# A half's worth of recurrence layers moved on by two in a fused recurrence and mixture-of-experts kernel on one core

## The chip, the cores and the metric

The kernel runs as one program on one core of a Trainium2 chip. The metric is the device time of one execution in microseconds (us); for several runs their median is given. Five engines work side by side, each on its own instruction stream: TensorE (PE in the profile; its weight loads are PEld), VectorE (DVE), ScalarE (ACT), GpSimd (POOL) and SyncE (SP), which here only issues DMA transfers. They wait for each other through semaphores.

## The reference

Two layers on `x` of 4 sequences x 1024 tokens x 1024 channels in float32. Each layer has a recurrence over the tokens (forwards and backwards) whose keys and values are both the `side` input and whose receptance is `x`, and a feed-forward part.

```python
# k = v = side, r = x; per channel: decay from w and cond
ek = exp(min(k, 30)); ekv = ek * v
a = a * decay + ekv_t          # numerator scan, forwards (nf) and backwards (nb)
b = b * decay + ek_t           # denominator scan (df, db)
euk = exp(min(u + k, 30))
num = nf + nb - ekv + euk * v
den = df + db - ek + euk
out = sigmoid(r) * num / max(den, 1e-8) * (0.8 + 0.2 * tf)

x = x + linear(recurrence_0(x, side)) # 1024x1024, scaled per output, with bias
r = recurrence_1(x, side)
h = rmsnorm(r) * norm_w
routed = top-4 of 32 experts on h (w1 1024x(2x512), silu(g) * u, w2 512x1024)
shared = (silu(h @ sg) * (h @ su)) @ sd
x = x + r + routed + shared
```

So num/den of both layers needs only `side`. The first layer's recurrence is also gated with `sigmoid(x)` of the input; the second one's sigmoid can only be applied when the first layer's x is known, so the kernel computes its quotient (called ratio) ahead of it.

## The kernel before, in words

**Products.** Every float32 product is made of three products of fp32r halves (a high and a low part of either operand). The 4096 tokens are worked off in eight *halves* of 512 tokens (`HALVES`). A half has 32 *steps* (`STEPS`); a step is one product of a 128-wide output block, 24 matmuls of 128x512. Steps 0, 1, 2, 4, 6, 8, 10, 11 (`STEP_L`) are the eight output blocks of the first layer's linear, steps 3, 5, 7, 9 and 12 to 15 (`STEP_D`) the eight blocks of the *previous* half's shared down product, steps 16 to 31 the gate and up products of the shared feed-forward. Half 0 has no previous half. `fill(h, i)` (L1482) is what an engine does in step i of half h. DVE's share is: at step_l(o)+1 the product's result is added to x (`XL`, L1505), at step_l(o)+2 the ratio is multiplied by the sigmoid (`C1`, L1498), at step_d(o)+1 the down product is taken in (`down`, L1455) and the residual sum is made (L1513). At step 16 the RMS root is taken (`root`, L1460 to L1468), then the eight blocks are normalised (`normalize`, L1477) and their low parts split (L1439); PE, which has summed the squares (L1696), transposes (L1706), computes the router's logits (L1708) and goes on with step 16.

**Recurrence layers.** The recurrences of both layers are cut into 32 *units*, a unit being one sequence and one block of 128 channels, 1024 tokens long; unit u is channel block u mod 8 of sequence u/8. A unit has two recurrence layers, l=0 (gated, written to `gated_dram`) and l=1 (ratio, written to `ratio_dram`), which share the side and its exponential EK and the product EKV = EK * side. A layer is on DVE: the denominator's forward scan F, the numerator's forward scan G, both backward scans, the term W = exp(u+k) in between, then two Newton operations on the inverse (which ACT starts by a Relu, Ln, Exp chain) and the scaling with it (`scaled`, L1094; with the gate multiply L1099 where l=0). POOL clips the side (L613), ACT takes its exponential (`side_exp`, L702).

**Order.** The order is written out by hand in `with_halves` (one list of calls per engine). The first eight units (`ALONE`) run in `alone`, before half 0 and next to the splitting of 32 pieces of shared weights on PE and ACT, four pieces a unit. There the EKV multiply is L1119, the scans are L1128, L1132, L1135 and L1145, the end of ACT's inverse chain is L833, L837, L839, and each unit's x is loaded to one buffer `X` by ACT's queue (L879) when the gate of the unit before is done. The other 24 units run in `unit`, four per half in halves 0 to 5 and always two halves ahead of their use: each unit's two layers are laid between eight steps of the half, with `fill(i)` calls at fixed places:

```python
for h in range(1, HALVES - 2):
    for q in range(UNITS_PER_HALF):
        u = h * UNITS_PER_HALF + ALONE + q
        unit(u, q % 2, lambda i: fill(h, q * FILLS_PER_UNIT + i, ...), prompt(u), not prompt(u - 1))
```

A *slot* below is one of the eight layers of a half, with four steps each; in DVE's `unit`, l=0 (even slots) has `fill(0)` ahead of the first scan and `fill(1)` behind it, l=1 has `fill(4)` behind its first scan and `fill(5)` only behind its scans and the scaling. The scaling is put off into the next layer, since the numerator's sum is made by an accumulating DMA that POOL issues (`add_numerator`); only the last unit of a sequence (`prompt`) scales at once. The next side is loaded by ACT's queue (`load_side`, L707) after the gate multiply of the layer before, x by L720.

**Half 6** has no units. DVE does the first part of the router's ranking there (`route_early`: `rank_start` at step 0, four `rank`s of six operations, L1242 to L1247, at steps 2, 4, 6, 8, the rest from step 19 on), and POOL then writes the routing entries as 112 small indirect DMAs (`put_entries`, L604) behind step 29 of half 6. Half 7 and the loop over the experts (L1822, L1836) follow.

## Time and profile before

| | |
|---|---|
| time, median of 3 runs (lowest, highest) | 4742.23 us (4740.93, 4744.61) |
| the profiled execution's own time | 4735.88 us |
| its span | 4734.2 us |
| its mean granted TensorE clock | 0.973 of full speed |
| PE busy | 4476.6 us (95%) |
| DVE busy | 2502.9 us (53%) |
| ACT busy | 1794.9 us (38%) |
| POOL busy | 834.6 us (18%) |

The profile is of one execution. The span runs from its first to its last instruction; the execution's own time is 1.7 us longer. Times in the rows are counted from the span's start. A busy share over the whole span is a mean over stages that are bound by different engines, so the section with the rows reads it by stage.

### The profile page before, as it was taken

Reading aid. Unit: us, or ns where it says so; the run is one execution under the profiler, and the core shown is the slowest. Engines: PE = TensorE matmul, PEld = TensorE weight load, DVE = VectorE, ACT = ScalarE, POOL = GpSimd, SP = SyncE. Lnnn points to the kernel's source line nnn. Section 1 sums busy time; section 2 is a strip of 40 time slices with the busy share of each in tenths; the row PEclk is TensorE's granted clock in tenths of the full one; section 3 lists DMA queues with packets and bytes.
Section 4 is the critical chain, followed back from the end, with each engine's and each line's share of the span. In section 5 each row is a group of like instructions: output and inputs, shape, how many; then the busy total and the mean of one; then the engine's idle time right before and its main releaser. Section 6 shows DMA issues by size and latency. Waiting matters only on the chain.

```text
span 4734.2 us, 60632 instructions
## 1 busy us (share of the span) xinstructions
PE 4476.6 (95%) x19926; PEld 3553.3 (75%) x19927; DVE 2502.9 (53%) x2708; ACT 1794.9 (38%) x2597; POOL 834.6 (18%) x992
## 2 busy tenths in 40 slices
PE   6778999999999946999999999999999999999999
PEld 2346787777778734778888888888888888888887
DVE  8999999999998411433143333444432143233432
ACT  6655555555554301232132323333331142222331
POOL 4410100101000062111111111111211111111211
PEclk9988999999999967999999999999999999999999
DMA  6777888988888624564254453655643345444443
GB/s 254 271 239 233 278 293 270 302 269 289 280 253 301 208 79 137 201 248 111 58 168 107 122 161 89 221 159 153 202 132 89 62 142 186 115 111 111 146 128 62
DMA packets 253977, 857.11 MB, mean 181 GB/s; under 512 B 28832, under 2 KB 61728, under 8 KB 229024
## 3 DMA queue, kind: packets, MB, share of 16 engines
q1 hardware_dynamic: 172944, 572.77, 34.1%
q0 software_dynamic: 53776, 182.09, 18.0%
q10 hardware_dynamic: 27136, 100.67, 5.6%
q8 instruction: 71, 1.16, 0.1%
q14 instruction: 50, 0.41, 0.0%
HBM read 652.40 MB, written 181.01 MB: 176 GB/s over the span
## 4 chain that ended last, share of the span: by engine, by line
PE 83%; issue 4%; DVE 3%; DMA 2%; ACT 0%; POOL 0%; POOLq 0%; DVEq 0%; ACTq 0%
PE ps L1822 33%; PE ps L1686 26%; PE ps L1836 16%; PE ps L1755 3%; PE ps L1708 1%; PE ps L1811 1%; PE ps L1696 1%; DMA work<-rows_dram,row_idx 1%; PE ps L1706 1%; PE ps L1722 1%; DVE halves L1558 0%; DVE work L1178 0%; DVE work L1195 0%; DVE work L1169 0%; DVE halves L1446 0%
## 5 line engine op out<-in xcount | busy, mean ns | idle before, releaser
L1822 PE MATMUL ps<-halves 128*128 128x512 f32 x7152 | 1695.5, 393 | 3.5 <-DVE halves L1563 2.8
L1686 PE MATMUL ps<-halves 128*128 128x512 f32 x6144 | 1469.6, 397 | 114.3 <-issue 106.2
L1822 PEld LDWEIGHTS ps<-halves 128*128 128x128 f32 x7152 | 1336.9, 189 | 278.4 <-DVE halves L1563 3.1
L1686 PEld LDWEIGHTS ps<-halves 128*128 128x128 f32 x6144 | 1159.2, 189 | 401.5 <-issue 159.0
L1836 PE MATMUL ps<-halves 128*128 128x512 f32 x3576 | 834.9, 389 | 1.3 <-DVE halves L1579 1.3
L1836 PEld LDWEIGHTS ps<-halves 128*128 128x128 f32 x3576 | 671.1, 188 | 140.9 <-DVE halves L1579 1.6
L1563 DVE TENSOR_TENSOR halves<-ps,halves 128x1024 fp32r<-128x1024 f32 x150 | 183.7, 1225 | 902.5 <-ACT halves L985 902.5
L594 POOL DMA_INDIRECT out<-work,add_idx x149 | 249.8, 1677 | 1420.4 <-DVE work L1585 1219.8
L1558 DVE TENSOR_TENSOR halves<-work,halves 128x1024 fp32r<-128x1024 f32 (+1 forms) x320 | 440.2, 1433 | 83.5 <-ACT halves L989 83.5
L985 ACT ACTIVATE halves<-ps 128x1024 fp32r<-128x1024 f32 x150 | 154.0, 1027 | 859.6 <-PE ps L1822 859.6
L989 ACT ACTIVATE halves<-work 128x1024 fp32r<-128x1024 f32 (+1 forms) x320 | 369.1, 1229 | 67.7 <-PE ps L1836 57.3
L1579 DVE TENSOR_TENSOR halves<-ps,halves 128x256 fp32r<-128x256 f32 x298 | 112.3, 419 | 491.5 <-ACT halves L1019 491.5
L1019 ACT ACTIVATE halves<-ps 128x256 fp32r<-128x256 f32 x298 | 98.6, 383 | 544.2 <-PE ps L1811 544.2
L1585 DVE TENSOR_SCALAR work<-ps,acc 128x512 f32<-128x512 f32 x149 | 111.6, 749 | 276.4 <-PE ps L1836 266.5
L1025 ACT ACTIVATE work<-ps,acc 128x512 f32<-128x512 f32 x149 | 102.1, 685 | 408.5 <-PE ps L1836 388.5
L613 POOL TENSOR_SCALAR work<-work 128x1024 f32<-128x1024 f32 x33 | 112.4, 3405 | 698.2 <-DMA work<-side_t 603.6
L584 POOL DMA_INDIRECT work<-rows_dram,row_idx x151 | 151.9, 1006 | 122.0 <-POOL row_idx L580 62.7
L1755 PE MATMUL ps<-ident,work 128*128 128x128 f32 x1200 | 158.4, 276 | 12.0 <-DMA work<-rows_dram,row_idx 12.0
L604 POOL DMA_INDIRECT slots_dram<-acc x128 | 124.5, 973 | 237.8 <-DVE acc L1319 199.4
L1755 PEld LDWEIGHTS ps<-ident,work 128*128 128x128 f32 x1200 | 137.8, 143 | 13.1 <-DMA work<-rows_dram,row_idx 13.0
L579 POOL COPY acc<-work (+1 forms) x151 | 48.9, 324 | 484.4 <-PE ps L1755 470.7
L696 ACT ACTIVATE work<-work,ones 128x512 f32<-128x512 f32 (+1 forms) x160 | 129.6, 810 | 5.2
(222 smaller groups left out, 3798.7 us busy)
## 6 DMA issues: line engine op xcount, KB each, us to landing
halves<-split_dram SPq DMA_DIRECT2D x512, 512.0 KB
work<-expert_w SPq DMA_DIRECT2D x192, 1024.0 KB, 5.6
split_dram<-halves ACTq DMA_DIRECT2D x32, 1024.0 KB, 5.2
plain<-shared_w SPq DMA_DIRECT2D x32, 512.0 KB, 3.4
work<-side_t ACTq DMA_DIRECT2D x32, 512.0 KB, 6.7
gated_dram<-work ACTq DMA_DIRECT2D x32, 512.0 KB, 5.1
work<-x_t ACTq DMA_DIRECT2D x32, 512.0 KB, 5.7
ratio_dram<-second ACTq DMA_DIRECT2D x32, 512.0 KB, 5.1
```

Source lines behind the costliest of these rows:

```text
L584: pool.indirect_dma_start(hx, None, rows_dram[:, :], bass.IndirectOffsetOnAxis(row_idx[:, :].bitcast(u32), 0)).then_inc(s["rows_in"], 16)
L594: pool.indirect_dma_start(out[:, :], bass.IndirectOffsetOnAxis(add_idx[:, :].bitcast(u32), 0), y, None, compute_op=ALU.add).then_inc(s["y_ ...
L604: pool.indirect_dma_start(slots_dram[:, :], bass.IndirectOffsetOnAxis(where[:, t * TOPK + k:t * TOPK + k + 1].bitcast(u32), 0), entry[:, 2 ...
L696: sc.activation(place, place, ACT.Ln, bias=ones[:, 0:1]).then_inc(s[steps], 1)
L985: sc.activation(xhi, ps_xt[:, :], ACT.Copy).then_inc(s["x_hi"], 1)
L989: sc.activation(whi[q][:, part], staged(q, part), ACT.Copy).then_inc(s["w1_hi" if q < 4 else "w2_hi"], 1)
L1558: ve.tensor_tensor(wlo[q][:, part], staged(q, part), whi[q][:, part].bitcast(f32), ALU.subtract)\
L1563: ve.tensor_tensor(xlo, ps_xt[:, :], xhi.bitcast(f32), ALU.subtract).then_inc(s["x_lo"], 1)
L1686: last = pe.matmul(bank(k % 4), w, op[:, part], start=(c == 0 and w is w_hi and op is hi), stop=(c == CB - 1 and w is w_lo))
L1755: last = pe.transpose(ps_xt[:, c * P:(c + 1) * P], hx[:, c * P:(c + 1) * P], ident[:, :])
L1822: last = pe.matmul(ps_h[:, a * 512:a * 512 + 512], xp[:, xk * P:(xk + 1) * P], wp[:, rhs], start=(xk == 0 and xp is xhi and wp is whi[q]), ...
L1836: last = pe.matmul(ps_y[:, h * 512:h * 512 + 512], ap_[:, (q * 2 + k) * P:(q * 2 + k + 1) * P], wp[:, rhs:rhs + 512], start=(q == 0 and k ...
```

## The change

The order of the recurrence layers becomes a table `JOBS` of (unit, layer). The unit is no longer the piece that is worked off, the layer (*job*) is.

- Fourteen jobs run before half 0, not sixteen: the second layers of units 4 and 5 are left out there. Every half takes eight jobs, in the slots 0 to 7: the second layers of the previous group's first two units (slots 0, 1), the first layers of this group's first two (2, 3), then both layers of the third (4, 5) and of the fourth (6, 7). The last two second layers run in steps 0 to 7 of half 6.
- A unit whose layers are apart has its side loaded, clipped and exponentiated twice (`SIDE_FIRST`): 46 times in all for 32 before. In slots 0 to 3 EK is multiplied in place into EKV (`single`, L1258), behind the first scan; elsewhere L1268 does it.
- Every job that opens a side has `fill(0)` ahead of and `fill(1)` behind its first scan; slots 5 and 7 keep the order of a second layer.
- Channel blocks 4 to 7 of a sequence are processed as 6, 7, 4, 5 (`UNIT_OF`, with the inputs permuted to match on the host), and the linear's contraction and `ratio_step` follow it.
- In the opening x has two buffers (`x_alone`), and is loaded a unit ahead; jobs 1, 3, 5 and 7 split three weight pieces, the other jobs two (`SPLIT_AT`).
- The ranks of half 6 move from steps 2, 4, 6, 8 to 12, 13, 14, 17 (`RANK_AT`), `rank_start` to step 11, the zeros' memset and store to steps 8 and 10.

```diff
+FILLS_PER_JOB = FILLS_PER_UNIT // 2
...
+LATE = UNITS_PER_HALF // 2
+UNIT_OF = (0, 1, 2, 3, 6, 7, 4, 5)
...
+def has_late_layer(u):
+
+    return u >= UNITS_PER_HALF and u % UNITS_PER_HALF < LATE
...
+JOBS = [(u, l) for u in range(ALONE) for l in range(2) if not (l and has_late_layer(u))]
+JOBS_ALONE = len(JOBS)
+JOBS_PER_HALF = 2 * UNITS_PER_HALF
+for first in range(ALONE, BLOCKS, UNITS_PER_HALF):
+    JOBS += [(first - UNITS_PER_HALF + q, 1) for q in range(LATE)]
+    JOBS += [(first + q, 0) for q in range(LATE)]
+    JOBS += [(first + q, l) for q in range(LATE, UNITS_PER_HALF) for l in range(2)]
+JOBS += [(BLOCKS - UNITS_PER_HALF + q, 1) for q in range(LATE)]
...
+SIDE_FIRST = [n for n, (u, l) in enumerate(JOBS) if l == 0 or has_late_layer(u)]
...
-    return STEP_L[o - 4] + 3 if o >= 4 else o // 2
+    return (STEP_L[0] + 3, STEP_L[1] + 3, STEP_L[5], STEP_L[7])[o - 4] if o >= 4 else o // 2
...
+RANK_AT = (12, 13, 14, 17)
...
+        def single(n):
+
+            return n >= JOBS_ALONE and slot(n) < 2 * LATE
...
+            for n in range(JOBS_ALONE):
+                u, l = JOBS[n]
+                if u < ALONE - 1:
+                    alone(n, lambda i: None)
+                else:
+                    alone(n, lambda i: fill(-1, STEPS - FILLS_PER_UNIT + i, first=False, prev=False, next_=True))
+            for n in range(JOBS_ALONE, len(JOBS)):
+                h, q = divmod(n - JOBS_ALONE, JOBS_PER_HALF)
+                job(n, lambda i: fill(h, q * FILLS_PER_JOB + i, first=h == 0, prev=h > 0, next_=True))
...
+                if l == 0 and u and not last:
+                    sc.wait_ge(s["gated"], u + 1)
+                    load_x(u + 1)
...
+                if l == 0 and has_late_layer(u):
+                    side_exp(SIDE_AT[n + 1])
...
+                def numerator_forward():
+                    if single(n):
+                        ve.wait_ge(s["h_fwd"], n + 1)
+                        ve.tensor_tensor(EK, EK, side, ALU.mult).then_inc(s["ekv"], 1)
...
+                if opens_side:
+                    fill(0)
+                    ve.wait_ge(s["ek"], i + 1)
...
+                ve.tensor_tensor_scan(F, d, EK, 0.0, ALU.mult, ALU.add).then_inc(s["h_fwd"], 1)
+                if prompt(n):
+                    numerator_forward()
+                else:
+                    fill(1 if opens_side else 0)
...
+                if not prompt(n):
+                    numerator_forward()
+                if pending(n):
+                    scaled(n - 1, W_of[1 - n % 2], N)
+                if prompt(n) or not opens_side:
+                    fill(1)
...
-                if i in (2, 4, 6, 8):
...
+                if i in RANK_AT:
```

What moves on DVE is seen in slot 3 of half 2, steps 12 and 13 (in the first order, of before, the second layer of the half's second unit). L1169 is the denominator's forward scan, L1178 its backward scan, L1167 the numerator's forward scan, L1094 and L1099 the scaling and the gate multiply of the layer before; L1498, L1505, L1455 and L1513 are the steps' work on PE's results.

```order
L1169 SCALAR_TENSOR_TENSOR work<-decay,work 128x1024
L1498 TENSOR_TENSOR plain<-work,more 128x512
L1505 SCALAR_TENSOR_TENSOR work<-ps,lsb,work 128x512
L1178 SCALAR_TENSOR_TENSOR work<-decay,edge_in,work 128x1024
L1167 SCALAR_TENSOR_TENSOR work<-decay,work 128x1024
L1094 SCALAR_TENSOR_TENSOR work<-work,neg_gain 128x1024
L1099 TENSOR_TENSOR work<-work 128x1024
L1455 TENSOR_TENSOR work<-ps,work 128x512
L1498 TENSOR_TENSOR plain<-work,more 128x512
L1513 SCALAR_TENSOR_TENSOR work<-work,lsb,plain 128x512
L1191 SCALAR_TENSOR_TENSOR work<-second,cap,work 128x1024
```

And in the changed kernel, where these are L1269, L1276, L1262, L1183, L1188, and L1591, L1598, L1548, L1606 for the steps' work; L1258 is the new multiply:

```order
L1269 SCALAR_TENSOR_TENSOR work<-decay,work 128x1024
L1548 TENSOR_TENSOR work<-ps,work 128x512
L1591 TENSOR_TENSOR plain<-work,more 128x512
L1606 SCALAR_TENSOR_TENSOR work<-work,lsb,plain 128x512
L1276 SCALAR_TENSOR_TENSOR work<-decay,edge_in,work 128x1024
L1258 TENSOR_TENSOR work<-work 128x1024
L1262 SCALAR_TENSOR_TENSOR work<-decay,work 128x1024
L1183 SCALAR_TENSOR_TENSOR work<-work,neg_gain 128x1024
L1188 TENSOR_TENSOR work<-work 128x1024
L1285 SCALAR_TENSOR_TENSOR work<-second,cap,work 128x1024
```

The three operations on a down product (L1455, L1498, L1513) stood behind both scans and the scaling; they (L1548, L1591, L1606) now stand right behind the first scan, and the multiply is added between the other two scans.

The second place is ACT's in the opening, behind a first layer of a unit. Before (L833 to L839 is the inverse, L715 the ratio's store, L798 a weight piece's high part, L815 and L821 the next layer's edges, L827 its exponential, L702 the exponential of the next unit's side):

```order
L833 ACTIVATE work<-ps,neg_low 128x1024
L837 ACTIVATE work<-work,low 128x1024
L839 ACTIVATE work<-work 128x1024
L715 DMA ratio_dram<-second 128x1024
L798 ACTIVATE halves<-plain 128x2x512 x2
L815 ACTIVATE edge_in<-work,edge 128x1
L821 ACTIVATE edge_in<-work,edge 128x1
L827 ACTIVATE work<-work,uu 128x1024
L702 ACTIVATE work<-work 128x1024
```

In the changed kernel behind job 9, the first layer of unit 5 (L942 to L948 is the inverse, L799 a result's store, L790 and L786 the loads of x and side, L781 the exponential of the side):

```order
L942 ACTIVATE work<-ps,neg_low 128x1024
L946 ACTIVATE work<-work,low 128x1024
L948 ACTIVATE work<-work 128x1024
L799 DMA gated_dram<-work 128x1024
L790 DMA work<-x_t 128x1024
L781 ACTIVATE work<-work 128x1024
L897 ACTIVATE halves<-plain 128x2x512 x2
L786 DMA work<-side_t 128x1024
L807 ACTIVATE edge_in<-work,edge 128x1
L815 ACTIVATE edge_in<-work,edge 128x1
```

The side's exponential stood in the next layer, behind its edges; it now stands behind the last operation of the inverse.

## Rows read from the trace of the kernel before

**Rows 1.** The busy tenths of the span in 40 slices, PE and DVE

```profile
PE   6778999999999946999999999999999999999999
...
DVE  8999999999998411433143333444432143233432
```

**Rows 2.** Busy time by stretch: us, PE, PEld, DVE, ACT, POOL (count), PEclk, DMA share, GB/s

```profile
17.90:286.40 268.50, 208.35 (x448) 89.54 (x449) 252.82 (x147) 174.06 (x196) 103.30 (x24) 0.92 0.71 264
286.40:480.30 193.90, 160.80 (x647) 119.40 (x646) 181.14 (x156) 112.58 (x157) 18.06 (x11) 0.90 0.71 233
...
1081.20:1282.60 201.40, 198.50 (x869) 155.17 (x869) 190.59 (x172) 117.81 (x167) 19.64 (x12) 1.00 0.84 282
...
1691.30:1827.10 135.80, 30.72 (x53) 14.89 (x53) 4.18 (x7) 4.67 (x7) 92.81 (x96) 0.52 0.09 24
...
591.00:680.60 89.60, 87.93 (x392) 72.44 (x390) 83.17 (x70) 52.87 (x74) 8.21 (x4) 1.00 0.86 295
680.60:778.70 98.10, 97.72 (x428) 77.96 (x429) 92.19 (x82) 54.30 (x75) 9.31 (x6) 1.00 0.88 287
```

**Rows 3.** Timelines of DVE, ACT, POOL, opening: start, us, operation, count [idle before]

```profile
144.69 1.20 DVE L1119 TENSOR_TENSOR work<-work 128x1024 f32<-128x1024 f32 x1
...
160.42 2.27 DVE L1128 TENSOR_TENSOR_SCAN work<-decay,work 128x1024 f32<-128x1024 f32 x1
...
164.79 3.06 DVE L1135 TENSOR_TENSOR_SCAN work<-decay,edge_in,work 128x1024 f32<-128x1024 f32 x1
...
209.55 1.20 DVE L1119 TENSOR_TENSOR work<-work 128x1024 f32<-128x1024 f32 x1
...
235.37 2.35 DVE L1135 TENSOR_TENSOR_SCAN work<-decay,edge_in,work 128x1024 f32<-128x1024 f32 x1 [5.64 <-ACT edge_in L815]
...
161.18 1.06 ACT L839 ACTIVATE work<-work 128x1024 f32<-128x1024 f32 x1
...
223.42 1.06 ACT L694 ACTIVATE work<-work 128x1024 f32<-128x1024 f32 x1 [5.98 <-DMA work<-x_t]
...
162.87 4.56 POOL L613 TENSOR_SCALAR work<-work 128x1024 f32<-128x1024 f32 x1 [14.36 <-DVE work L1128]
```

**Rows 4.** Timeline of DVE, half 0, where steps 7 and 8 meet

```profile
333.46 0.69 DVE L1498 TENSOR_TENSOR plain<-work 128x512 f32<-128x512 f32 x1 [2.27 <-issue]
```

**Rows 5.** Timeline of DVE, half 2, from step 13's slot to the normalised blocks

```profile
753.82 2.34 DVE L1178 TENSOR_TENSOR_SCAN work<-decay,edge_in,work 128x1024 f32<-128x1024 f32 x1
...
760.69 0.68 DVE L1455 TENSOR_TENSOR work<-ps,work 128x512 f32<-128x512 f32 x1
...
770.39 1.28 DVE L1205 SCALAR_TENSOR_TENSOR work<-work,low 128x1024 f32<-128x1024 f32 x1 [1.73 <-ACT work L754]
...
774.24 0.68 DVE L1460 TENSOR_SCALAR work<-ps 128x512 f32<-128x512 f32 x1
...
777.22 1.41 DVE L1477 SCALAR_TENSOR_TENSOR work<-plain,nrm,work 128x512 f32<-128x512 f32 x2
```

**Rows 6.** Timeline of PE, half 2: behind step 12, and at the transposes

```profile
758.42 1.02 PE L1696 MATMUL ps<-work,ones 128*128 128x512 f32 x2
...
778.72 0.60 PE L1706 MATMUL ps<-ident,work 128*128 128x128 f32 x4
```

**Rows 7.** Timelines of ACT's queue and POOL, half 2: side load and clip for slot 4

```profile
761.18 0.50 ACTq L707 DMA_DIRECT2D work<-side_t  x1
...
768.41 2.88 POOL L613 TENSOR_SCALAR work<-work 128x1024 f32<-128x1024 f32 x1 [21.63 <-DMA work<-side_t]
```

**Rows 8.** DVE and PE in half 6: a rank's last operation; DVE busy time; PE's transposes

```profile
1515.20 0.96 DVE L1247 SCALAR_TENSOR_TENSOR work<-work 128x768 f32<-128x768 bf16 x1
...
1554.80:1575.80 21.00, 5.59 (x8) 1.00 0.57 173
...
1580.82 0.38 PE L1706 MATMUL ps<-ident,work 128*128 128x128 f32 x2
```

**Rows 9.** Timeline of POOL, half 6, the first of the indirect stores

```profile
1670.75 1.06 POOL L604 DMA_INDIRECT slots_dram<-acc  x1 [47.21 <-DVE acc L1319]
```

714 lines of the change are left out of this document (366 added, 348 removed).

## The prediction, made before the changed kernel was run

> **What bounds the kernel now.** I read the busy tenths of the span first, then the busy table by stage, then the timelines of VectorE (DVE), TensorE (PE) and ScalarE (ACT) around the places that the new order touches. In the tenths the reader sees PE below full and DVE at nine at the start, both near full up to slice 12, and PE alone from slice 16 on [rows 1]. The table by stage says where the regimes change [rows 2]. The opening, 17.9 to 286.4 us, holds the 16 layers of the first eight units: DVE is busy for 252.8 of 268.5 us, so DVE sets its length. Half 0 (286.4 to 480.3) has no down products, so PE has little to do in its first part and DVE, 181.1 of 193.9 us, sets it as well. Halves 1 to 5 read alike: half 4 takes 201.4 us with PE busy 198.5, so PE sets it. But DVE is busy 190.6 us there, so it has only some 11 us to spare, and what counts is whether they lie where the new order wants them. Then comes a stretch of 135.8 us in which PE issues only 53 matmuls while GpSimd (POOL) issues its small scattered stores; I come back to it last. The expert part behind 2062 us is not touched.
>
> **What the change removes: two layers from the opening.** The four layers of two units run from one EKV multiply at 144.69 to that of the next unit but one at 209.55, 64.9 us [rows 3]. Of such four in units 4 and 5, the two first layers stay. Their length is no longer DVE's alone. Formerly the exponential of the next unit's side stood in the second layer, early; now it stands behind the last exponential of the first layer (the second listing of the change). DVE would be through with that layer at 160.42, but ACT ends its last exponential at 161.18 + 1.06 [rows 3], and the side's, 1.06 more, comes behind it, so the next EKV multiply starts at 163.3: 18.6 us a layer, 37.2 for two. Job 10 then finishes a first layer in place of a second one and carries its gate multiply, 1.2 us like the EKV multiply. 64.9 - 37.2 - 1.2 = **26.5 us less**. A second gain lies in the x loads: at 235.37 DVE has stood idle for 5.64 us behind ACT, because ACT had waited 5.98 us for x until 223.42 [rows 3]. Now x has two buffers and is issued a unit ahead, which removes that. In exchange, x and side of units 5 and 6 have one layer's time to land, not two, while the first weight pieces load; I bound what that costs by 0 and the old 5.6, and take 2, nearer to 0 because a side load took 7.2 us to its clip in half 2 [rows 7] and a layer is 18.6 long. **3.6 us less.** The third weight piece that jobs 1, 3, 5 and 7 now split adds two copies of about 1 us to ACT, which is busy for 174.1 of 268.5 us there [rows 2]: nothing, and 2 us for each of the four if that cover were gone. Opening: -30.1 us, with ends of -22 and -34.
>
> **What it adds to each half.** The side is now opened six times per half, not four: two more loads of 512 KB, two more clips on POOL, two more exponentials on ACT and two more multiplies on DVE, 1.2 us each. The first listing of the change shows how DVE's work stands. Before, only slots 0 and 2 of a half's first sixteen steps took in PE's results behind the first scan; slots 1 and 3 did so only behind the scans and the scaling. Now all of slots 0 to 3 take them in early. In steps 0 to 15 DVE gains two EKV multiplies (slots 1 and 3) and loses the gate multiply of slot 1, whose layer now follows a second layer: one in sum, 1.15 us from start to start; in steps 16 to 31 it is one as well.
>
> *Half 0.* DVE sets steps 0 to 15, so everything is added. The multiply is 1.15. Where one job's last step meets the next job's first without a scan between, DVE waits for ACT's sigmoid: 2.27 us at 333.46 [rows 4]. That now happens at three transitions in place of one: 4.5 more. Two more clips lengthen a DVE scan beside them, 3.06 in place of 2.27 us [rows 3]; I take one of the two as felt, 0.8. Sum **+6.5 us**, ends 2 and 10.
>
> *Halves 1 to 5.* Here the added work itself would fit, but its place does not. Step 13's work needs PE's product of step 12, which ends at 758.42 in half 2 [rows 6]. In the profile DVE had by then done the scans and the scaling and took it in at 760.69; now it stands before them. DVE went from the backward scan at 753.82 to the RMS root at 774.24 in 20.4 us, 1.73 of them idle at 770.39 [rows 5]. The same work plus the multiply now starts with step 13's at 758.5: 20.4 - 1.7 + 1.15 = 19.8 us, and the root starts at 778.3. The first normalised block is ready 3.7 us behind the root's start (777.22 + 0.7 before), at 782.0; PE arrives at its transposes at 778.72 [rows 6] and waits 3.3 us. Before, it waited for nothing there, with less than 1 us to spare. PE's idling may cost clock too: half 0, where PE stands for 33 us, has a granted clock of 0.90, half 4, with 3 us of it, 1.00 [rows 2]; taken in proportion that is 19 us for 30, 2 us for 3.3, and I take a third of it, 0.7, because one wait is not a stretch of many. **4.0 us a half, +20.0 for five**; ends 0 (DVE finds the time elsewhere) and 6. The multiply added behind the transposes costs nothing while DVE waits for PE in that part: in half 1 DVE ran for 83.2 of 89.6 us between transposes and end [rows 2]; were that cover gone, it would be 1.2 a half. The ratio of the last block is now stored in slot 2 and loaded at step 11 for step 13. In half 2 of before that is some 19 us behind the same point of DVE's work, against a store and a load of which the load takes 7.2 [rows 7]: nothing. The accumulate that POOL issues stands behind a clip as before.
>
> *Half 6* gets two jobs where DVE had the first ranks to do; they run like slots 0 and 1 of any half, without a wait of PE. The ranks move to steps 12 to 14 and 17. A rank is six operations like the one of 0.96 us at 1515.20, 5.9, the first with a copy 0.6 more: 18.3 us for three ahead of the root. Between the product taken in at 1554.8 and the root at 1575.8, DVE is busy for 5.6 of 21.0 us, so 15.4 take them in and the root is 2.9 late. The first block then follows 3.7 behind it, and PE, which had 5.0 (1580.82) [rows 8], waits 1.6: **+1.6 us**, ends 0 and 6.
>
> *The slow stretch.* POOL's stores start at 1670.75 [rows 9], PE falls from 1691.3 on to 53 matmuls in 135.8 us, one in 2.6, and that is over at 1827.1 [rows 2]. What releases them (step 29 of half 6) stays where it is, so I cost it at nothing; the lead of 20.6 us before PE suffers is the bound on both sides.
>
> **Sum:** -30.1 + 6.5 + 20.0 + 1.6 = -2.0 us against the profiled execution's own 4735.88 us. The median of the runs is 6.35 us above that, 4742.23, so I expect **4740 us**. The change moves the work out of a stretch that DVE sets, and most of it comes back as waits of PE in six stretches. A measurement of this kernel can tell about 0.2%, 9.5 us, from no change.
>
> **Rivals.** *The place costs little (faster).* If DVE finds 2 us for its added multiply and clip and the operations behind the new place overlap better, PE waits 1.2 us a half, and half 0 adds only 2: -30.1 + 2 + 6 + 1.6 = -20.5 gives 4722 us. For it: DVE had 5.9 us of idle time in the 98.1 us up to half 2's transposes [rows 2]. Against it: step 12's product is PE's own pace, which no spare time moves. The Trainium skill (Perfetto Trace Analysis, Optimization Strategy) says that where the most contended engine changes over time, interleaving the regimes may improve the kernel; taken at its word that is this rival, 4722 us. The rows agree that the engine changes [rows 2] and speak against the full gain by the 19.8 us chain. Chance 0.29.
>
> *ACT's new wait in front of the transposes (slower).* The side for slot 4 is now loaded only after the gate of slot 2, at about 768.9 in half 2, against 761.18. ACT takes its exponential before it splits the normalised blocks. With 7.2 us to landing, 2.9 for the clip [rows 7] and 1.1 for the exponential it ends at 780.1, 1.9 before it matters. It decides from a landing of 9.1 us on. At 12 us, each of five halves loses 3 more: 4755 us. Chance 0.13.
>
> *Port contention (slower).* If each of the 12 clips added in halves 0 to 5 stopped DVE for its whole 2.9 us [rows 7], not for the 0.8 of the lengthened scan, that is 12 x 2.1 more: 4765 us. The Trainium skill (SBUF — State Buffer, SBUF: two separate sides) states that the port pair of DVE and GpSimd is an exclusive lock for a whole instruction, the other one being fully blocked. The scan at 164.79 beside the 4.56 us clip of 162.87 grew by 0.8 us only [rows 3], so the trace does not bear that out. Chance 0.05.
>
> *The slow stretch moves.* Should PE's shorter program put its start 20 us earlier or later against the stores, the time is 4760 or 4720. Chance 0.04 each.
>
> **Numbers.** The forecast has 0.45, within 4731 to 4749; the range that leaves out no more than 0.2 is 4718 to 4757. Faster by over 0.2%, below 4732.7, takes 0.29 + 0.04 and 0.01 of the forecast's own lower end, 0.34; slower 0.13 + 0.05 + 0.04, 0.22; the rest, 0.44, is within.
>
> **What would show it.** Right: half 0's first product near 256 us in place of 286.4; halves of 204 to 205 us, with PE waiting 3 to 4 us for DVE in front of its transposes (the group ps<-ident,work at its first of 32), DVE waiting for PE ahead of step 13; half 0 near 200 us; root to transposes unchanged. Wrong: a half that still takes 201 us (then the first rival), an ACT wait for POOL just ahead of the split of the normalised blocks (then the second), an opening that shrinks by under 20, or a slow stretch of another length than 136 us.

## The result, and the profile after

The changed kernel takes 4763.05 us (median of 5; 4762.31 to 4769.23) against 4741.2 us (median of 5) for the kernel before on the same chip: ratio 1.0052, interval 1.0040 to 1.0063. It is 22 us slower. The prediction had 4740 us and a range up to 4757. Two of its rivals lie near 4763: contention of POOL and DVE at 4765, and a slow stretch that starts 20 us earlier or later against the stores at 4760. Neither is what happened: without any clip in the halves the change still costs (the run without clips below), and the slow stretch begins 19.3 us behind POOL's first store (1719.50 against 1700.18) where it began 20.6 us behind it before. The profiled execution took 4769.04 us, its span 4767.3 us, 33.1 us more than the span before. The two profiled executions thus lie further apart than the medians, 33 against 22 us; the stages below are read from them, and c_before and c_after further on give the same stages a second time.

The busy tenths of the changed kernel show the same regimes as [rows 1], with PE's hole a little later, since everything up to it is longer:

```profile
PE   7769999999999955999999999999999999999999
...
DVE  8999989989889621433142342533532143333432
```

The stages tell more. This is the busy table by stretch of the changed kernel (us, then PE, PEld, DVE, ACT, POOL with counts, PEclk, DMA share, GB/s): the opening, half 0 up to its transposes, then halves 1 to 6, each cut at the first logits matmul of its transposes, and the slow stretch.

```profile
17.90:255.90 238.00, 191.19 (x416) 81.48 (x417) 223.64 (x131) 165.26 (x185) 88.12 (x22) 0.93 0.80 295
255.90:355.90 100.00, 60.69 (x214) 42.18 (x212) 92.04 (x75) 55.32 (x74) 17.40 (x8) 0.78 0.60 192
355.90:564.30 208.40, 202.10 (x866) 156.07 (x865) 189.43 (x166) 117.11 (x163) 27.27 (x14) 0.98 0.80 269
564.30:774.80 210.50, 202.55 (x870) 157.20 (x870) 192.20 (x172) 119.17 (x167) 26.05 (x12) 0.98 0.78 270
774.80:986.10 211.30, 202.13 (x870) 156.86 (x869) 189.37 (x169) 118.70 (x165) 28.24 (x14) 0.98 0.83 274
986.10:1196.00 209.90, 201.12 (x870) 155.93 (x869) 191.49 (x168) 118.06 (x164) 24.90 (x12) 0.99 0.79 271
1196.00:1410.30 214.30, 202.45 (x869) 156.91 (x868) 189.72 (x169) 118.92 (x167) 26.54 (x14) 0.98 0.80 270
1410.30:1610.50 200.20, 198.49 (x870) 155.26 (x870) 178.75 (x176) 99.36 (x144) 13.10 (x7) 1.00 0.78 269
1719.00:1855.00 136.00, 30.52 (x54) 14.72 (x52) 4.18 (x7) 4.68 (x7) 94.37 (x98) 0.51 0.11 31
```

The same view of the kernel before, cut at the same places, gave:

```profile
286.40:379.70 93.30, 60.20 (x215) 42.63 (x213) 89.12 (x74) 53.48 (x72) 10.01 (x6) 0.81 0.65 205
379.70:578.70 199.00, 198.65 (x865) 154.93 (x864) 184.68 (x165) 115.03 (x162) 19.75 (x12) 0.99 0.84 278
...
1382.80:1581.40 198.60, 198.26 (x870) 155.28 (x870) 151.71 (x162) 88.92 (x132) 8.55 (x5) 1.00 0.76 257
```

Stage by stage: the opening ends at 255.9 in place of 286.4 [rows 2], 30.5 us less. Half 0 takes 100.0 in place of 93.3 us to its transposes, 6.7 more. Halves 1 to 5 together take 1054.4 us (355.9 to 1410.3) in place of 1003.1 (379.7 to 1382.8), 51.3 more, or 10.3 each. Half 6 takes 200.2 in place of 198.6, 1.6 more. The slow stretch is as long as it was. -30.5 + 6.7 + 51.3 + 1.6 is 29.1 of the span's 33.1 us; the last 4 lie behind half 6. Of these 3.0 lie behind half 7's logits, in code that the change does not touch; it took 2825.4 to 2830.6 us in all profiled executions here but one (e9_no_multiply, which routes other tokens), in no order that goes with the edits. So the question is one: why did a half grow by 10 us where 4.0 were forecast?

PE's timeline of the changed kernel in half 2 shows where PE stands (start, us, operation, count, [idle before]):

```profile
755.17 1.13 PE L1786 MATMUL ps<-work,ones 128*128 128x512 f32 x2 [1.49 <-ACT work L1005]
755.73 6.05 PE L1776 MATMUL ps<-halves 128*128 128x512 f32 x24
765.35 0.63 PE L1812 MATMUL ps<-ident,work 128*128 128x128 f32 x4 [3.57 <-ACT work L988]
765.82 1.40 PE L1786 MATMUL ps<-work,ones 128*128 128x512 f32 x2
766.28 7.68 PE L1776 MATMUL ps<-halves 128*128 128x512 f32 x24
773.79 0.60 PE L1812 MATMUL ps<-ident,work 128*128 128x128 f32 x4
774.23 0.60 PE L1796 MATMUL ps<-ident,work 128*128 128x128 f32 x4
```

PE comes to its transposes (L1796) without a wait. It stood before: 1.49 us for ACT's square (L1005) and 3.57 us for ACT's copy (L988) of the bank through which finished output blocks are turned. And behind that wait the 24 matmuls of a step take 7.68 us, not 6.05. The busy table says why: the first 3.8 us of them ran at a granted clock of 0.55, which is the lower of its two levels, 1.2 GHz, for nearly all of that time.

```profile
766.20:770.00 3.80, 3.80 (x10) 2.61 (x9) 3.73 (x5) 1.74 (x3) 2.75 (x1) 0.55 0.29 82
```

Counted over halves 1 to 5, the time from the last 96 product matmuls' start to the first logits matmul (the last four steps) grew from 26.4 to between 33.6 and 35.1 us, 7.7 us of the 10.3. Another 1.5 lies in steps 0 to 3, where PE stops at the half's first step, and 0.7 in steps 4 to 7. DVE's timeline of the same half:

```profile
703.03 2.35 DVE L1276 TENSOR_TENSOR_SCAN work<-decay,edge_in,work 128x1024 f32<-128x1024 f32 x1 [4.19 <-ACT edge_in L807]
...
722.62 0.69 DVE L1591 TENSOR_TENSOR plain<-work 128x512 f32<-128x512 f32 x1 [1.62 <-ACT work L777]
...
746.36 0.69 DVE L1591 TENSOR_TENSOR plain<-work,more 128x512 f32<-128x512 f32 x1 [2.27 <-issue]
...
749.83 0.67 DVE L1548 TENSOR_TENSOR work<-ps,work 128x512 f32<-128x512 f32 x1
...
759.81 1.28 DVE L1285 SCALAR_TENSOR_TENSOR work<-second,cap,work 128x1024 f32<-128x1024 f32 x1
...
769.74 0.68 DVE L1553 TENSOR_SCALAR work<-ps 128x512 f32<-128x512 f32 x1
```

Two waits are new in kind. The first is slot 1's: the backward scan waits 4.19 us for ACT's copy of the scan's last column (L807). The others are the transitions from slot to slot, 1.62 and 2.27 us here (a third of 1.62 at 694.65). In steps 0 to 15 DVE's waits add up to 9.7 us. In the kernel before they were 5.3: 1.73 us for ACT's part of the inverse, ahead of a Newton operation [rows 5], 0.40 us at another such place, and this one for PE:

```profile
729.17 0.69 DVE L1455 TENSOR_TENSOR work<-ps,work 128x512 f32<-128x512 f32 x1 [3.13 <-PE ps L1722]
```

ACT's timeline in the changed kernel says why they grew:

```profile
702.11 0.63 ACT L1005 ACTIVATE work<-plain 128x512 f32<-128x512 f32 x1 [6.55 <-PE ps L1786]
702.65 0.28 ACT L807 ACTIVATE edge_in<-work,edge 128x1 f32<-128x1 f32 x1
...
761.21 1.15 ACT L836 ACTIVATE work<-work,neg_low 128x1024 f32<-128x1024 f32 x1 [3.33 <-DVE work L1285]
...
764.63 0.58 ACT L988 ACTIVATE work<-ps 128x512 f32<-128x512 f32 x1
...
771.03 1.06 ACT L781 ACTIVATE work<-work 128x1024 f32<-128x1024 f32 x1 [2.42 <-POOL work L693]
```

In slot 1 ACT now does the slot's first step ahead of the edge copy, and in that step lies a square that waits for PE's sums. At a transition the sigmoid that DVE waits for starts when DVE's L1598 of the step before has ended. In slot 3 the bank copy (L988) stands behind the inverse chain (L836 and on), which waits for DVE's L1285. The side's exponential (L781) does wait for POOL, 2.42 us, but ends before the blocks to be split are there.

### The profile page after: what moved, and what is told of

It is laid out like the page before. It is cut to its first block, busy times and chain, and to the rows that moved or that the text cites. A ratio compares the mean times of both kernels' runs of the same rounds, so it can differ in the third digit from the quotient of the medians.

```text
span 4767.3 us, 60710 instructions
## 1 busy us (share of the span) xinstructions
PE 4476.3 (94%) x19892; PEld 3549.3 (74%) x19895; DVE 2532.6 (53%) x2725; ACT 1812.9 (38%) x2610; POOL 870.4 (18%) x1004
## 4 chain that ended last, share of the span: by engine, by line
PE 64%; issue 3%; DVE 1%; DMA 1%; ACT 0%; POOL 0%; POOLq 0%; DVEq 0%; ACTq 0%
PE ps L1912 33%; PE ps L1926 16%; PE ps L1776 10%; PE ps L1845 3%; PE ps L1901 1%; DMA work<-rows_dram,row_idx 1%; DVE halves L1649 0%; PE ps L1798 0%; PE ps L1786 0%; PE ps L1796 0%; PE ps L1812 0%; ACT halves L1072 0%; DMA out<-work,add_idx 0%; DVE work L1676 0%; DVE work L1548 0%
## 5 line engine op out<-in xcount | busy, mean ns | idle before, releaser
L693 POOL TENSOR_SCALAR work<-work 128x1024 f32<-128x1024 f32 x46 | 156.7, 3407 | 944.5 <-DMA work<-side_t 510.9
L1598 DVE SCALAR_TENSOR_TENSOR work<-ps,lsb,work 128x512 f32<-128x512 f32 x64 | 47.4, 740 | 164.0 <-remote 132.3
```

Of the source, the lines that this page charges most:

```text
L693: pool.tensor_scalar(EK, side_buffer(n), 30.0, None, ALU.min).then_inc(s["kc"], 1)
```

## The experiments

All further runs were made on four other chips, on which the kernel before takes 4608 to 4610 us. To have both kernels there, they were run again unedited. The first four expectations count from the first chip's 4741 and 4763 us, so of them the differences are what can be compared. The theories: A, the bank copy in ACT's queue is the wait; B, DVE has one chain ahead of the transposes, with too much work in it; C, POOL's clips; D, ACT's edge copy behind a step in slot 1; E, formed after the first eight runs, the orders of DVE and ACT must match, and what DVE loses is its waits for ACT.

> The kernel before, unedited, on this chip, for its trace: the opening up to 286 us and halves of 201 us as shown, and no crawl of PE behind the indirect stores of half 6, so that the 130 us between this chip's time and the other's are that stretch alone.

> The changed kernel itself, unedited, on the chip of the other experiments, on which the kernel before takes 4609.6 us. All theories: the same 1.005 against before, 4632 us; halves of 210 us again, and, as in the experiments before it, no stretch in which PE crawls. If the crawl were the change's own cost, the ratio would be 1.000 here.

The kernel before: 4611.08 us in its own run, 4609.82 over ten. The changed kernel: 4636.25 us, ratio 1.0054 (1.0040 to 1.0068). The change costs the same here. The crawl of PE is absent in both, so it has no part in the difference; more on it in the last section. The stages agree: opening 31.3 us shorter, half 0 6.7 longer, halves 1 to 5 1054.0 in place of 1005.9 us (9.6 each), half 6 1.8 longer. The runs below are compared with these two by this table, whose lengths are read from PE's timelines, from half 0's first product to its first logits matmul, then from logits matmul to logits matmul.

| run | time, us | ratio to before | half 0, front | halves 1 to 5 | half 6 |
|---|---|---|---|---|---|
| c_before | 4611.1 | 1 | 93.3 | 1005.9 | 198.5 |
| c_after | 4636.3 | 1.0054 | 100.0 | 1054.0 | 200.3 |
| e1_copy_early | 4637.7 | 1.0058 | 99.9 | 1049.5 | 200.4 |
| e2_fill_order | 4657.9 | 1.0100 | 103.5 | 1073.1 | 200.4 |
| e3_no_clip | 4623.9 | 1.0028 | 96.8 | 1045.6 | 200.1 |
| e4_before_x_twice | 4604.5 | 0.9988 | 92.9 | 1006.1 | 198.5 |
| e5_enter_first | 4639.7 | 1.0063 | 103.3 | 1053.2 | 200.8 |
| e7_all_three | 4625.2 | 1.0034 | 100.2 | 1038.8 | 200.1 |
| e8_scan_first | 4598.9 | 0.9981 | 93.2 | 1020.6 | 201.0 |
| e9_no_multiply (other routing, see there) | 4594.9 | 0.9972 | 94.9 | 1037.5 | 200.5 |
| e10_before_multiply | 4616.2 | 1.0018 | 95.8 | 1010.9 | 198.8 |
| e11_scan_first_only | 4597.9 | 0.9973 | 93.2 | 1020.4 | 200.5 |
| e12_second_step_late | 4587.8 | 0.9949 | 92.5 | 1017.0 | 200.3 |

**The bank copy alone.**

```diff
-COPY_AT = (6, 8, 10, 12, 14, 15, 17, 18)
+COPY_AT = (6, 8, 10, 12, 13, 15, 17, 18)
```

> The changed kernel with one number changed: ACT copies the fifth output block out of its one bank at step 13, ahead of its inverse chain, not at step 14, behind it. Theory A (the bank copy is the wait: PE stands 3.6 to 4.1 us in steps 14/15 of halves 1 to 5 only because the copy is queued behind the inverse, and runs the next 24 matmuls slower): the wait goes and nothing takes its place, 5.5 us in each of five halves, about 4736 us. Theory B (DVE's chain is late and the bank is only where PE meets it): PE reaches its transposes 4 to 5 us earlier and waits there for DVE's first normalised block, some 3 us; 1 to 2 us a half are left, about 4755 us.

No change in the total: 1.0058 (1.0044 to 1.0072). Halves 1 to 5 get 0.9 us shorter each, and between the transposes of halves 6 and 7 1.5 us are added. In half 2 of this run PE stands at the same place, now for DVE:

```profile
753.21 1.12 PE L1786 MATMUL ps<-work,ones 128*128 128x512 f32 x2 [2.00 <-ACT work L1005]
...
762.74 1.11 PE L1812 MATMUL ps<-ident,work 128*128 128x128 f32 x4 [2.92 <-DVE work L1548]
```

So the bank was only where PE met a late DVE: theory A falls. Theory B's wait of 3 us is there, though at the output block and not, as expected, at the first normalised block.

**DVE's order of before in slots 1 and 3, ACT's left as changed.**

```diff
                 if opens_side:
-                    fill(0)
+                    if not late_fill:
+                        fill(0)
...
-                    fill(1 if opens_side else 0)
+                    fill(1 if opens_side and not late_fill else 0)
...
-                if prompt(n) or not opens_side:
+                if prompt(n) or late_fill or not opens_side:
                     fill(1)
```

> The changed kernel with DVE's slots 1 and 3 in the order of before: the slot's first step behind the first scan, its second behind scans and scaling. Theory B (in the new order DVE's work on PE's results of two neighbouring steps stands back to back and DVE waits for ACT's sigmoid at each transition, 2.27 or 1.62 us, and does step 13's work ahead of the scans): these waits shrink to one a half, the sums' and the bank's waits of PE go, halves come down from 210 to 203 us or less, 4725 us. Theory A (ACT's queue alone): the order on DVE matters only in so far as the inverse can start earlier; the sums' wait of 1.5 us stays and the halves fall by 3 to 4 us, 4745 us.

The opposite of what either theory expected: 22 us slower than the changed kernel. PE's timeline of half 1:

```profile
552.96 1.11 PE L1814 MATMUL ps<-ident,work 128*128 128x128 f32 x4 [8.24 <-DVE work L1550]
```

DVE now starts a slot with a scan that needs the side's exponential, which ACT does last in the slot before: DVE waits 3.24 us for it in slots 1 and 3, and again for the edge copy. This order on DVE costs time with ACT's order left as it is. Both put back together, as the kernel before has them, was not run.

**No clip.**

```diff
                 n = SIDE_FIRST[i]
+                if n >= JOBS_ALONE:
+                    return
                 pool.wait_ge(*side_landed(i))
...
+                if n >= JOBS_ALONE:
...
+                    sc.activation(EK, side_buffer(n), ACT.Exp).then_inc(s["ek"], 1)
```

> The changed kernel without POOL's clip of the side at 30 in the halves (all 32 clips there are left out; ACT takes the exponential straight from the loaded side, whose values lie far below 30). Theory C (POOL's clips lengthen DVE's work beside them and stand ahead of the accumulating DMAs and of ACT's exponential): by the operation that took 2.06 us for 1.28 beside a clip, 0.8 us each, two or three of them felt a half, 2 us a half, 4751 us; with a whole clip of 3.6 us lost each time it would be 12 us a half and 4700 us. Theories A and B: under 5 us in all, 4760 us.

The edit leaves out all 38 clips behind the opening (46 less the opening's 8; the expectation says 32), and with them ACT's waits for POOL. 12 us less than the changed kernel: 3.2 in half 0, 8.4 in halves 1 to 5, 1.7 each. That is theory C's 2 us a half, far from a whole clip each time. How much of it is contention and how much ACT's waits for POOL, the run does not tell apart.

**Two buffers for x, in the kernel before.**

```diff
+        x_alone = (X, RES[:, 0:SEQ])
...
+                    sc.wait_ge(s["gated"], u + 1)
+                    sc.dma_start(x_alone[(u + 1) % 2], x_t[(u + 1) * P:(u + 2) * P, :]).then_inc(x_sem[(u + 1) % 2], 16)
...
-                sc.dma_start(X, x_t[(u + 1) * P:(u + 2) * P, :]).then_inc(s["x_in"], 16)
```

> The kernel before with one part of the change alone: two buffers for x in the opening, each x load issued a unit ahead. All theories: the wait of 5.64 us of DVE at 235.37 goes, the opening gets 5 to 6 us shorter and half 0 starts near 281 us; everything behind is unchanged but for the slow stretch, which may move. 4736 us. If x was not what ACT waited for, the opening stays at 286 us and the time at 4741 us.

4604.46 us, ratio 0.9988 (0.9979 to 0.9997); half 0 starts at 281.45 for 285.79. DVE's wait at this place was 5.64 us on the first chip and is 4.46 in c_before. It is gone, and 4.3 us of the 4.46 are gained.

**ACT's order of before in slots 1 and 3, DVE's left as changed.**

```diff
-                if opens_side:
+                early = part in (1, 3) and not prompt(n)
+                if opens_side and not early:
                     fill(0)
                 enter(n, F)
...
                 third_exp()
+                if early:
+                    fill(0)
```

> The changed kernel with ACT's order of before in slots 1 and 3: the copy of the scan's last column and the layer's exponential stand ahead of the slot's first step, not behind it. Theory D (in slot 1 that step holds a square that waits for PE, ACT waited 6.55 us there in half 2 and DVE's backward scan 4.19 us behind it, and all of DVE's later waits of PE follow from this): DVE's wait goes, PE's waits at the sums and the bank shrink from 5 to under 2 us a half, halves of 206 us, 20 us in all. Theory B (DVE simply has too much work in front of the transposes; the wait only fills time that it has): the wait turns up again behind PE and the halves stay within 1 us of 210.

No gain (1.0063). DVE's wait at the edge is gone in half 2, but two rows of DVE's timeline there show it again in slot 3:

```profile
745.22 0.69 DVE L1594 TENSOR_TENSOR plain<-work,more 128x512 f32<-128x512 f32 x1 [2.27 <-issue]
...
752.78 0.69 DVE L1594 TENSOR_TENSOR plain<-work,more 128x512 f32<-128x512 f32 x1 [3.42 <-ACT work L777]
```

ACT has moved the step's sigmoid behind the edge and the exponential, and DVE, which wants it first, waits 3.42 us. This is the counterpart of the run with DVE's order of before: ACT's order of before, alone, gains nothing. Theory D falls as stated.

**All three.** The two edits and no clip:

> The changed kernel with three edits: ACT's order of before in slots 1 and 3, the fifth block's bank copy a step earlier, and no clip by POOL in the halves (left out, as in the run without clips). If their gains add up (20, 5 and 14 us), this is 40 us under the changed kernel, some 20 us under the kernel before, faster than both. If one chain on DVE stands behind all three, the sum is 25 us or less, and it is about level with before.

4625.18 us, 11 us under the changed kernel and no more than the clips alone gave. Against the gains that were expected, 20, 5 and 14 us, that is a miss. Against those that the three runs measured it is not: in halves 1 to 5 they gave 0.8, 4.5 and 8.4 us, 13.7 together, and all three give 15.2; in half 0 they gave -3.3, 0.1 and 3.2, and all three give -0.2. So the three add up, and what fell is the size of two of them.

**Both engines together.** DVE's scan ahead of the slot's first step, the second step right behind the second scan, and on ACT the edge and the exponential ahead of the first step and the next side's exponential ahead of the slot's last; with the early bank copy.

```diff
+                ahead = slot(n) in (1, 2, 3) and not prompt(n) and n < len(JOBS) - 2
                 if opens_side:
-                    fill(0)
+                    if not ahead:
+                        fill(0)
...
-                    fill(1 if opens_side else 0)
+                    fill(1 if opens_side and not ahead else 0)
...
+                if ahead:
+                    fill(1)
                 if not prompt(n):
                     numerator_forward()
...
+                exp_ahead = part in (0, 1, 2) and not prompt(n) and n < len(JOBS) - 3
+                if exp_ahead:
+                    side_exp(SIDE_AT[n + 1])
                 fill(3)
```

> The changed kernel with a third order of slots 1 to 3 and the early bank copy: on DVE the slot's first scan stands ahead of its first step and its second step right behind the second scan; on ACT the scan's last column and the layer's exponential stand ahead of the first step, and the next side's exponential ahead of the slot's last step. Theory E (what DVE loses is its waits for ACT: 1.6 + 4.6 + 1.6 + 2.3 us in steps 0 to 15 of half 3, 10 us, against 4 in the kernel before; a scan that covers each sigmoid takes them away, if all go at once): halves of 203 us, 40 us less than the changed kernel, 4597 us, faster than before. Theory B (DVE has one chain from PE's step 12 to the root, and PE waits for its end): under 2 us a half, 4628 us or more.

4598.87 us, ratio 0.9981 (0.9972 to 0.9990): 37 us under the changed kernel, and under the kernel before. All the added work is still done; only its order differs. The halves fall by 6.7 us each, the front of half 0 by 6.8, all by which it had grown. Theory E expected this, and theory B under 2 us a half. The edit moves four things at once, two on DVE and two on ACT; none of them was run alone, so what each is worth is not shown.

**DVE's added work.** The first run leaves out the multiply in slots 0 to 3. The numerator is then another one and other tokens are routed; the part behind half 7 takes 2807.5 us, some 20 less than in the other runs. So the total of this run says nothing, and only its halves are compared. The second adds the same multiply to the kernel before:

```diff
-                        ve.tensor_tensor(EK, EK, side, ALU.mult).then_inc(s["ekv"], 1)
+                        ve.sem_inc(s["ekv"], 1)
```

> The changed kernel without the multiply EK * side in slots 0 to 3 (left out; the numerator's scan runs over EK there, so that what is routed changes and only the halves are compared, by their length from transposes to transposes). Theory B (DVE's work in steps 0 to 15 is what PE waits for): four times 1.23 us of work gone, halves shorter by 3 to 5 us of the 9.6 by which they grew. Theory E (ACT's part of the chain): by 0 to 2 us.

```diff
+                        if l == 1:
+                            ve.wait_ge(s["h_fwd"], n + 1)
+                            ve.tensor_tensor(EKV, EK, side_of[par], ALU.mult).then_inc(s["again"], 1)
...
```

> The kernel before with the multiply EK * side done a second time in every second layer (same values; two in steps 0 to 15 of a half, one or two behind), the added DVE work of the change alone, without its order, its loads and its clips. If DVE's busy time alone makes the halves long: 2.3 us or more a half in front of the transposes, 12 to 20 us in all, 4625 us. If the old order still has room for it (DVE waits 3.0 + 2.7 us for PE there, and PE came to its transposes without a wait): up to 1 us a half, 4612 us.

Taken from the changed kernel, 4.9 us of multiplies a half give 3.3 us a half. That is theory B's figure (3 to 5), not theory E's (0 to 2). Put into the kernel before, three or four multiplies a half, two of them (2.5 us) ahead of the transposes, cost 1.0 us a half, and 2.5 in half 0. So neither theory holds alone: work on DVE ahead of the transposes costs most of its length once DVE is late, and under half while the order leaves room, and the order decides which of the two it is.

**What of it is which.** Order alone, without the early bank copy; then with the second step of slots 1 to 3 late, where slot 3 had it before:

```diff
-                if ahead:
-                    fill(1)
...
-                if prompt(n) or not opens_side:
+                if prompt(n) or ahead or not opens_side:
                     fill(1)
```

> The run with the scan first (4598.9 us) without its early bank copy: order alone. That copy put 1.2 us of PE's waiting for ACT into every half, halves 6 and 7 too, which have no layers. If DVE now reaches the transposes early enough, the copy behind the inverse costs nothing: the 1.2 us go in seven halves, 4590 us, 0.4% under the kernel before. If it is still too late for the bank, PE stands there again for 1 to 3 us and it is 4600 us or more.

> As the run before it, but on DVE the second step of slots 1 to 3 stands behind scans and scaling, as slot 3 had it in the kernel before. The prediction held that the early place of step 13's work costs 3 to 4 us a half: then this is faster, by 15 us or more. If the early place is what PE's next step needs (with the late place and ACT's old order PE stood 8.2 us for that step's down product), it is slower, by 5 us or more a half, 4620 us and up.

4597.88 us (0.9973, interval 0.9962 to 0.9984) and 4587.84 us (0.9949, interval 0.9935 to 0.9963). The first lies between the two values that were expected, 4590 and 4600. The bank copy was worth nothing either way: in half 2 its 1.21 us went, and 1.44 us for the first normalised block came. The second is 10 us faster, not 15 or more. The late place of the second step gives 3.4 us in halves 1 to 5 and 0.7 in half 0. Of the rest of the 8.8 us between the two profiled executions, 4.0 lie behind half 7, which scatters by as much without an edit. In the last four steps of a half the late place gives more, 26.5 to 27.1 us for 28.5, and some of it is lost again around the half's first step. The last run is 22 us faster than the kernel before and 48 faster than the change, the fastest of all that were run. Half 3 by the busy table, in the kernel before, the changed one and this one (one line of each):

```profile
779.70:982.00 202.30, 200.03 (x869) 156.35 (x868) 184.74 (x166) 116.17 (x164) 18.58 (x12) 0.99 0.87 280
```

```profile
773.00:984.40 211.40, 201.16 (x870) 156.04 (x870) 189.84 (x167) 118.53 (x165) 26.96 (x14) 0.99 0.82 274
```

```profile
751.40:956.80 205.40, 200.32 (x870) 156.13 (x869) 187.88 (x168) 118.26 (x167) 27.25 (x14) 0.99 0.85 282
```

And its PE at the end of step 15 of half 2, where 3.57 and 1.49 us of waiting had been, with DVE's taking in of step 13 (L1556, at 732.89) and its root (L1561):

```profile
743.88 6.05 PE L1784 MATMUL ps<-halves 128*128 128x512 f32 x24
749.77 0.60 PE L1820 MATMUL ps<-ident,work 128*128 128x128 f32 x4
750.79 0.66 PE L1804 MATMUL ps<-ident,work 128*128 128x128 f32 x4 [0.42 <-DVE work L1578]
```

```profile
732.89 0.69 DVE L1556 TENSOR_TENSOR work<-ps,work 128x512 f32<-128x512 f32 x1
...
747.01 0.68 DVE L1561 TENSOR_SCALAR work<-ps 128x512 f32<-128x512 f32 x1
```

## Why the prediction was wrong

**Right.** The opening: -30.1 forecast, -30.5 measured. Its parts: x in two buffers, forecast 3.6, gave 4.3 in the kernel before, on another chip; that leaves 26.2 for the two layers, forecast 26.5. The EKV multiply behind job 8 starts at 164.30, behind ACT's exponential at 163.21 as forecast. The forecast had it at 163.3, 18.6 us behind the multiply before it; that one stands at 146.40, so the layer takes 17.9 us:

```profile
164.30 1.23 DVE L1213 TENSOR_TENSOR work<-work 128x1024 f32<-128x1024 f32 x1 [2.19 <-ACT work L781]
```

Half 0: +6.5 forecast, +6.7 measured, with 2.27 us of DVE's waiting at each of three transitions (282.46, 305.61, 328.75) in place of one, as priced. The split is not the forecast's, so the closeness of the sum is in part luck: DVE is busy for 2.9 us more, where 1.95 were forecast, and waits for 3.8 more, not 4.5. Half 6: +1.6 forecast, +1.6 measured, and most of it as a wait for the first normalised block, 1.37 us at 1609.88:

```profile
1609.88 0.66 PE L1796 MATMUL ps<-ident,work 128*128 128x128 f32 x4 [1.37 <-DVE work L1570]
```

Halves 1 to 5: the length of DVE's chain from step 13's work to the root: 19.8 us forecast, 19.9 measured (749.83 to 769.74). The slow stretch kept its length, and its distance from the stores to 1.3 us. ACT's late exponential ends at 772.09, ahead of the first block's split at 773.49, and decided nothing. POOL's clips cost 1.7 us a half in all.

**Wrong: the term "4.0 us a half, +20.0 for five", which measured 10.3 and 51.3.** With it the forecast of no change failed. Three things failed in it; what each is worth by itself the runs show only in part.

The first is the start of the chain. The working let it begin with PE's end of step 12 ("from 758.5", 746.7 in the changed kernel). It began at 749.83, 3.1 us later, since DVE first had to wait 2.27 us for ACT's sigmoid at the transition from slot 2 to slot 3, and has the slot's first scan to do behind it. A wait at the end of the chain that the forecast had at 3.3 us becomes 6.4 by this, on an estimate from these rows; that accounts for most of the 7.7 us of the last four steps. DVE's wait for the sigmoid had been found and priced, but in half 0 only: "That now happens at three transitions in place of one". For halves 1 to 5 it was left at nothing, because a half that PE sets seemed to have room. It hadn't, in front of the transposes.

The second is ACT. The listing of DVE's order was compared row by row; ACT's order in the same slots was not. It had changed as well: the edge copy of slot 1 went behind a step whose square waits for PE, and cost DVE 4.19 us in half 2. No sentence of the prediction has it. That the order costs the time is shown, since with the same work in a third order on both engines the halves fall by 6.7 us (-37 us in all, and -48 with the second step late). That it takes both engines is argued from two other edits: DVE's order of before alone gave +22 us, ACT's alone nothing. The third order was not run on one engine alone. And order is not all of it: leaving out DVE's multiplies gave 3.3 us a half as well.

The third is where PE meets a late DVE. The prediction looked at the transposes alone, where PE had less than 1 us to spare. But PE meets DVE and ACT at every sum and every turned block, and in the changed kernel it stood at those, 1.5 + 3.6 to 4.1 us. The longer stop is followed by slower matmuls in all five halves, 6.66 to 7.92 us for 6.05, 0.6 to 1.9 us where the forecast had put 0.7 for the clock. Behind the stop of 1.5 us they take 6.02 to 6.05.

The claim that the early place of step 13's work costs time was right in sign and mis-sized as the cause: 0.7 us a half between the last two runs (1.9 in the last four steps), not 3 to 4. The forecast had nothing for the clips in halves 1 to 5; all of them, old and new, gave 1.7 us a half. In half 0 it had 0.8 us for the two new ones, where all four gave 3.2. Its reading of the lengthened scan, 3.06 for 2.27 us, sets a backward scan beside a forward one; a backward scan without a clip takes 2.35 [rows 3], so it is 0.7.

The rule that interleaving may help where the most contended engine changes (the Trainium skill, Perfetto Trace Analysis, Optimization Strategy) was given 4722 us. The change as made does not bear it out, since it lost more in the halves than the opening gave. The last run does: with the same two layers moved, in an order that makes PE wait less, it is 0.5% faster. 0.1% of that is the second buffer for x, which needs no interleaving.

Left open: half 3 still takes 3 us more in the last run than in the kernel before. PE stands there for 1.75 and 2.73 us around the half's first step (853.66, 860.31), against 1.92 us at one place in c_before; why was not taken apart.

## What to carry to other kernels

When work is moved between stages, compare the order on every engine that takes part in the moved piece, not only on the one that sets the stage, and follow each instruction that stands ahead of a hand-over: does it wait for the engine that will end up waiting? A wait that was found in one stage has to be priced in every stage where the same order runs. And where two engines hand over to each other many times in a row, try orders for both at once: here one edit on each engine alone gave nothing or a loss, and another order, on both, 37 to 48 us.

## What the runs showed of the hardware

**PE's crawl came with the first chip and not with the kernel.** On the first chip, PE issued 53 matmuls in 135.8 us at a granted clock of 0.52 while POOL issued its small indirect stores [rows 2, 9], and 54 in 136.0 in the changed kernel. On the four other chips the same instructions ran beside the same stores, without a trace of it. The kernel before on such a chip, the same stretch:

```profile
1691.30:1827.10 135.80, 135.46 (x593) 103.33 (x592) 49.48 (x92) 43.64 (x71) 99.52 (x98) 1.00 0.73 217
```

593 matmuls in place of 53, at full clock, with POOL as busy as before. This is what makes the kernel 4610 us there and 4741 here: from half 6's first logits matmul to half 7's it takes 199.4 us there and 326.9 here, 127.5 of the 131. What differs between the chips was not found out.

**A stop of PE can cost more than its length.** Behind 3.57 us of waiting 24 matmuls took 7.68 us in place of 6.05 (755.73 and 766.28 above): 1.6 us more, at a granted clock of 0.55 over the first 3.8 us. The ten stops of 3.6 to 4.3 us at this place in the two profiles of the changed kernel were followed by 0.5 to 1.9 us more; the ten of 1.5 us ahead of them by nothing. The granted clock of halves 1 to 5 is 0.98 to 0.99, against 0.99 to 1.00 before.

**A clip on POOL lengthens one DVE operation beside it by some 0.8 us, not by its own 3.6.** In half 2 of the changed kernel the clip runs from 709.03 to 712.64. Of the two like operations beside it one takes 2.06 us in place of 1.28 and the next its usual 1.27, though the clip still runs when it starts:

```profile
709.92 2.06 DVE L1285 SCALAR_TENSOR_TENSOR work<-second,cap,work 128x1024 f32<-128x1024 f32 x1
711.90 1.27 DVE L1286 SCALAR_TENSOR_TENSOR second<-second,cap,work 128x1024 f32<-128x1024 f32 x1
```

```profile
709.03 3.61 POOL L693 TENSOR_SCALAR work<-work 128x1024 f32<-128x1024 f32 x1 [20.03 <-DVE work L1262]
```

Over all 46 clips of that profile, the DVE operations beside a clip together took at most 0.83 us more than the same operations do as a rule (their median), and 0.56 us on average. The Trainium skill (SBUF — State Buffer, SBUF: two separate sides) has the loser of the port pair fully blocked. Leaving out all clips of a half, six of them, gave 1.7 us, so the runs do not show such a block.
